# New written orders of all engines in the first five and the last iterations of a two-layer graph-attention kernel

## What is computed

```python
# layer 0
q, k, v = x @ Wq + bq, x @ Wk + bk, x @ Wv + bv
attn = softmax(where(adj == 0, -inf, q k^T / sqrt(32)))
y = (attn v) @ Wo + bo + x
x = layernorm(y) * gamma + beta
# layer 1
nx = layernorm(x) * ln1_g + ln1_b
q, k, v = nx @ wq + bq, nx @ wk + bk, nx @ wv + bv
bias = where(adj > 0, 0.1 * adj * adj, -inf)
attn = softmax(q k^T / sqrt(32) + bias)
x1 = x + (attn v) @ wo + bo
n2 = layernorm(x1) * ln2_g + ln2_b
out = x1 + gelu(n2 @ w1 + b1) @ w2 + b2
```

## Time and profile before

| what | value |
|---|---|
| median of 3 runs | 2076.92 us |
| the profiled execution's own time | 2076.95 us |
| its span, first to last instruction | 2075.2 us |
| TensorE busy | 2028.0 us, 98% |
| VectorE, ScalarE busy | 1655.5 and 1654.2 us, 80% each |
| GpSimd busy | 1005.0 us, 48% |
| mean granted clock of TensorE | 0.99 |
| DMA, mean rate | 35 GB/s |

### The profile page before, as it was taken

One profiled execution on the slowest core, in us unless ns is written; L12 is line 12 of the kernel. 1 busy time (PEld: TensorE's weight loads), 2 busy tenths in 40 slices (PEclk: granted clock), 3 DMA queues, 4 the chain that ended last, 5 costly groups with the idle time before them and its releaser, 6 DMA issues.

```text
span 2075.2 us, 57260 instructions
## 1 busy us (share of the span) xinstructions
PE 2028.0 (98%) x19008; PEld 1782.2 (86%) x19008; DVE 1655.5 (80%) x7107; ACT 1654.2 (80%) x5512; POOL 1005.0 (48%) x780
## 2 busy tenths in 40 slices
...
DMA packets 80830, 73.16 MB, mean 35 GB/s; under 512 B 3024, under 2 KB 72272, under 8 KB 80720
## 3 DMA queue, kind: packets, MB, share of 16 engines
...
q10 hardware_dynamic: 144, 0.01, 0.0%
...
## 4 chain that ended last, share of the span: by engine, by line
PE 96%; DVE 3%; issue 1%; DMA 1%; ACT 0%; SPq 0%; POOL 0%; ACTq 0%; DVEq 0%
PE ps L509 52%; PE ps L519 11%; PE ps L491 11%; PE ps L479 7%; PE ps L502 6%; PE ps L518 5%; PE ps L531 3%; PE ps L521 1%; DVE pm L939 1%; DVE xy L1036 0%; DMA m<-in_adj 0%; DMA xTr<-in_xT 0%; DVE stats L1021 0%; PE ps L463 0%; DVE actl L982 0%
## 5 line engine op out<-in xcount | busy, mean ns | idle before, releaser
L703 ACT ACTIVATE pm<-pm,nmax 128x128 f32<-128x128 f32 x2048 | 793.0, 393 | 97.8 <-DVE nmax L939 97.3
L1180 POOL TENSOR_TENSOR pm<-pm,rinv 128x512 f32<-128x512 f32 x512 | 524.1, 1044 | 715.8 <-DVE rinv L955 715.7
L939 DVE CUSTOM_DVE_ANT_0 pm<-ps,m 128x128 f32<-128x128 f32 x2048 | 452.9, 283 | 21.4 <-PE ps L479 16.0
L703 ACT ACTIVATION_READ_ACCUMULATOR pm<-pm,nmax 128x1 f32 x2048 | 392.7, 192 | 0.0
L519 PE MATMUL ps<-w,hh 128*128 128x512 f32 x1024 | 363.4, 399 | 2.5 <-DVE hl L1043 2.4
L491 PE MATMUL ps<-ident,pm 128*128 128x128 f32 x2048 | 288.9, 277 | 2.7 <-DVE nmax L939 1.9
L491 PEld LDWEIGHTS ps<-ident,pm 128*128 128x128 f32 x2048 | 236.7, 142 | 32.9 <-issue 3.4
L713 ACT ACTIVATE pt<-ps 128x512 f32<-128x512 f32 x256 | 151.2, 591 | 128.4 <-PE ps L491 128.3
L518 PE MATMUL ps<-w,hl 128*128 128x256 f32 x896 | 249.9, 279 | 0.0
L962 DVE COPY pt<-ps 128x512 f32<-128x512 f32 x256 | 169.2, 679 | 66.4 <-PE ps L491 66.2
L519 PEld LDWEIGHTS ps<-w,hh 128*128 128x128 f32 x1024 | 188.0, 188 | 39.1 <-DVE hl L1043 3.1
...
## 6 DMA issues: line engine op xcount, KB each, us to landing
...
```

Source lines behind the costliest of these rows:

```text
L703: last = nc.scalar.activation(pm[:, g, h, :], pm[:, g, h, :], ACT.Exp, bias=nmax[:, g, h:h + 1], scale=-1.0, accum_out=rsum[:, g, h:h + 1])
L939: last = nc.vector.tensor_tensor_reduce(out=pm[:, g, h, :], in0=src[:, at:at + N], in1=m[:, g, :], scale=1.0, scalar=3e38, op0=ALU.add, op ...
L1180: tt(pm[:, g, hs, :], pm[:, g, hs, :], rinv[:, g, hs].rearrange("p (h a) -> p h a", a=1).to_broadcast([P, HC, N]), ALU.mult).then_inc(norm ...
```

## The change

Only orders change. `body(i)`, `JOBS` and every helper stay as they are, as does all of SyncE's program. `head()` and `tail()` of TensorE, ScalarE, VectorE and GpSimd hold the same calls as before in another order, and `HEAD` and `TAIL` follow TensorE's. No instruction is added or removed. The parts of the diff that the prediction speaks of (a deleted and an added run of lines stand apart where lines between them are left out):

```diff
@@ -586,39 +585,39 @@
-                qkv(X, 0, 4); scores(X, 0, 1); flip(X, 0, 0, 0); flip(X, 0, 0, 1); qkv(X, 0, 5); second_products(0)
+                qkv(X, 0, 4); qkv(X, 0, 5); scores(X, 0, 1); flip(X, 0, 0, 0); flip(X, 0, 0, 1); second_products(0)
...
-                qkv(Y, 0, 1); flip(X, 1, 1, 0); qkv(Y, 0, 2); qkv(Y, 0, 3); qkv(Y, 0, 4); scores(Y, 0, 0)
+                flip(X, 1, 1, 0); qkv(Y, 0, 1); qkv(Y, 0, 2); qkv(Y, 0, 3); qkv(Y, 0, 4); scores(Y, 0, 0)
...
-                values(X, 1, 0); values(X, 1, 1); out_proj(X, 1, 0); scores(Y, 0, 1); qkv(X, 2, 0); out_proj(X, 1, 1)
+                values(X, 1, 0); values(X, 1, 1); out_proj(X, 1, 0); scores(Y, 0, 1); out_proj(X, 1, 1); qkv(X, 2, 0)
...
-                flip(Y, 0, 3, 0); flip(Y, 0, 3, 1); values(Y, 0, 0); values(Y, 0, 1); flip_rows("T1", 1, 0)
-                scores(X, 2, 1); flip_rows("T1", 1, 1); flip(X, 2, 0, 0); out_proj(Y, 0, 0); out_proj(Y, 0, 1)
-                flip(X, 2, 0, 1); qkv(Y, 1, 0); qkv(Y, 1, 1); qkv(Y, 1, 2); flip(X, 2, 1, 0); qkv(Y, 1, 3)
+                flip(Y, 0, 3, 0); flip(Y, 0, 3, 1); values(Y, 0, 0); values(Y, 0, 1); scores(X, 2, 1)
+                flip_rows("T1", 1, 0); out_proj(Y, 0, 0); flip(X, 2, 0, 0); flip_rows("T1", 1, 1); flip(X, 2, 0, 1)
+                out_proj(Y, 0, 1); qkv(Y, 1, 0); flip(X, 2, 1, 0); qkv(Y, 1, 1); qkv(Y, 1, 2); qkv(Y, 1, 3)
...
@@ -637,27 +636,27 @@
...
-                mlp_up(29, 3); mlp_up(29, 4); values(X, 31, 0); values(X, 31, 1); mlp_up(29, 5); mlp_up(29, 6)
-                mlp_up(29, 7); out_proj(X, 31, 0); out_proj(X, 31, 1); scores(Y, 30, 1); flip(Y, 30, 0, 0)
-                mlp_down(29, 0); mlp_down(29, 1); flip(Y, 30, 0, 1); flip(Y, 30, 1, 0); mlp_down(29, 2)
...
+                mlp_up(29, 6); out_proj(X, 31, 0); mlp_up(29, 7); scores(Y, 30, 1); out_proj(X, 31, 1)
+                flip(Y, 30, 0, 0); mlp_down(29, 0); mlp_down(29, 1); mlp_down(29, 2); flip(Y, 30, 0, 1)
+                flip(Y, 30, 1, 0); flip(Y, 30, 1, 1); mlp_down(29, 3); flip(Y, 30, 2, 0); flip(Y, 30, 2, 1)
...
@@ -762,36 +761,36 @@
-                x_hi(0, 0); x_hi(0, 1); q_out(X, 0, 0); q_out(X, 0, 1); copy_wo(0); k_out(X, 0, 0); k_out(X, 0, 1)
-                exp(X, 0, 0, 0); exp(X, 0, 0, 1); exp(X, 0, 1, 0); exp(X, 0, 1, 1); copy_pt(X, 0, 0); exp(X, 0, 2, 0)
-                exp(X, 0, 2, 1); exp(X, 0, 3, 0); exp(X, 0, 3, 1); copy_pt(X, 0, 1); copy_pt(X, 0, 2)
-                copy_pt(X, 0, 3); out_hi(X, 0, 0); x_hi(1, 0); x_hi(1, 1); out_hi(X, 0, 1); copy_w2(0); q_out(X, 1, 0)
...
+                x_hi(0, 0); x_hi(0, 1); copy_wo(0); q_out(X, 0, 0); q_out(X, 0, 1); k_out(X, 0, 0); k_out(X, 0, 1)
+                exp(X, 0, 0, 0); exp(X, 0, 0, 1); exp(X, 0, 1, 0); exp(X, 0, 1, 1); copy_pt(X, 0, 0); x_hi(1, 0)
+                exp(X, 0, 2, 0); exp(X, 0, 2, 1); exp(X, 0, 3, 0); exp(X, 0, 3, 1); copy_pt(X, 0, 1); copy_pt(X, 0, 2)
+                x_hi(1, 1); copy_pt(X, 0, 3); out_hi(X, 0, 0); out_hi(X, 0, 1); copy_w2(0); k_out(X, 1, 0)
...
-                out_hi(X, 1, 0); exp(Y, 0, 1, 0); exp(Y, 0, 1, 1); x_hi(2, 1); out_hi(X, 1, 1); exp(Y, 0, 2, 0)
...
+                out_hi(X, 1, 0); x_hi(2, 1); exp(Y, 0, 1, 0); out_hi(X, 1, 1); exp(Y, 0, 1, 1); exp(Y, 0, 2, 0)
...
@@ -1045,63 +1044,64 @@
-                x_lo(0, 0); x_lo(0, 1); split_kv(0, 1); first_rows(0); mask0(0); split_kv(0, 2)
...
-                mask_scores(X, 0, 2, 1); mask_scores(X, 0, 3, 0); split_qkv1(0, 0); recip(X, 0, 2)
-                mask_scores(X, 0, 3, 1); copy_pt(X, 0, 0); v_out(X, 0, 1); recip(X, 0, 3); second_shifts(0)
-                copy_pt(X, 0, 1); copy_pt(X, 0, 2); split_qkv1(0, 1); copy_pt(X, 0, 3); out_lo(X, 0, 0); x_lo(1, 0)
-                x_lo(1, 1); out_lo(X, 0, 1); residual("WO0", 0, 0); mask0(1); residual("WO0", 0, 1); norm_stats(0, 0)
-                norm_rows(0, 0); mask_scores(X, 1, 0, 0); mask_scores(X, 1, 0, 1); mask_scores(X, 1, 1, 0)
-                mask_scores(X, 1, 1, 1); norm_stats(1, 0); v_out(X, 1, 0); v_out(X, 1, 1); recip(X, 1, 0)
-                norm_rows(1, 0); mask_scores(X, 1, 2, 0); lo("T1", 0, 0); lo("T1", 0, 1); recip(X, 1, 1)
-                mask_scores(X, 1, 2, 1); mask_scores(X, 1, 3, 0); copy_pt(X, 1, 0); split_w1(0, 0); recip(X, 1, 2)
-                mask_scores(X, 1, 3, 1); split_w1(0, 1); v_out(Y, 0, 0); mask_scores(Y, 0, 0, 0); recip(X, 1, 3)
-                mask_scores(Y, 0, 0, 1); mask_scores(Y, 0, 1, 0); flipped(X, 1, 1, 1); mask_scores(Y, 0, 1, 1)
-                copy_pt(X, 1, 1); copy_pt(X, 1, 2); copy_pt(X, 1, 3); v_out(Y, 0, 1); out_lo(X, 1, 0); recip(Y, 0, 0)
-                x_lo(2, 0); mask0(2); residual("WO0", 1, 0); recip(Y, 0, 1); x_lo(2, 1); mask_scores(Y, 0, 2, 0)
-                out_lo(X, 1, 1); mask_scores(Y, 0, 2, 1); mask_scores(Y, 0, 3, 0); residual("WO0", 1, 1)
-                recip(Y, 0, 2); norm_stats(0, 1); mask_scores(Y, 0, 3, 1); norm_rows(0, 1); mask_scores(X, 2, 0, 0)
-                mask_scores(X, 2, 0, 1); flipped(Y, 0, 1, 0); mask_scores(X, 2, 1, 0); recip(Y, 0, 3)
-                copy_pt(Y, 0, 0); flipped(Y, 0, 1, 1); mask_scores(X, 2, 1, 1); copy_pt(Y, 0, 1); norm_stats(1, 1)
-                copy_pt(Y, 0, 2); copy_pt(Y, 0, 3); recip(X, 2, 0); norm_rows(1, 1); v_out(X, 2, 0); v_out(X, 2, 1)
...
+                x_lo(0, 0); x_lo(0, 1); first_rows(0); mask0(0); split_kv(0, 1); split_kv(0, 2)
...
+                mask_scores(X, 0, 2, 1); mask_scores(X, 0, 3, 0); mask_scores(X, 0, 3, 1); split_qkv1(0, 0)
+                recip(X, 0, 2); copy_pt(X, 0, 0); v_out(X, 0, 1); second_shifts(0); recip(X, 0, 3); copy_pt(X, 0, 1)
+                copy_pt(X, 0, 2); x_lo(1, 0); copy_pt(X, 0, 3); mask0(1); x_lo(1, 1); out_lo(X, 0, 0); out_lo(X, 0, 1)
+                split_qkv1(0, 1); residual("WO0", 0, 0); residual("WO0", 0, 1); norm_stats(0, 0); norm_rows(0, 0)
+                mask_scores(X, 1, 0, 0); mask_scores(X, 1, 0, 1); mask_scores(X, 1, 1, 0); mask_scores(X, 1, 1, 1)
+                norm_stats(1, 0); v_out(X, 1, 0); v_out(X, 1, 1); norm_rows(1, 0); recip(X, 1, 0)
+                mask_scores(X, 1, 2, 0); recip(X, 1, 1); lo("T1", 0, 0); lo("T1", 0, 1); mask_scores(X, 1, 2, 1)
+                mask_scores(X, 1, 3, 0); split_w1(0, 0); split_w1(0, 1); recip(X, 1, 2); mask_scores(X, 1, 3, 1)
+                copy_pt(X, 1, 0); v_out(Y, 0, 0); mask_scores(Y, 0, 0, 0); recip(X, 1, 3); mask_scores(Y, 0, 0, 1)
+                mask_scores(Y, 0, 1, 0); flipped(X, 1, 1, 1); mask_scores(Y, 0, 1, 1); copy_pt(X, 1, 1)
+                copy_pt(X, 1, 2); copy_pt(X, 1, 3); v_out(Y, 0, 1); out_lo(X, 1, 0); mask0(2); x_lo(2, 0)
+                recip(Y, 0, 0); x_lo(2, 1); residual("WO0", 1, 0); out_lo(X, 1, 1); recip(Y, 0, 1)
+                mask_scores(Y, 0, 2, 0); mask_scores(Y, 0, 2, 1); residual("WO0", 1, 1); norm_stats(0, 1)
+                recip(Y, 0, 2); mask_scores(Y, 0, 3, 0); mask_scores(Y, 0, 3, 1); norm_rows(0, 1); copy_pt(Y, 0, 0)
+                mask_scores(X, 2, 0, 0); mask_scores(X, 2, 0, 1); flipped(Y, 0, 1, 0); mask_scores(X, 2, 1, 0)
+                recip(Y, 0, 3); flipped(Y, 0, 1, 1); mask_scores(X, 2, 1, 1); copy_pt(Y, 0, 1); v_out(X, 2, 0)
+                norm_stats(1, 1); copy_pt(Y, 0, 2); copy_pt(Y, 0, 3); norm_rows(1, 1); v_out(X, 2, 1); recip(X, 2, 0)
+                out_lo(Y, 0, 0); mask_scores(X, 2, 2, 0); lo("T1", 1, 0); out_lo(Y, 0, 1); mask_scores(X, 2, 2, 1)
+                residual("WO1", 0, 0); recip(X, 2, 1); lo("T1", 1, 1); mask_scores(X, 2, 3, 0); residual("WO1", 0, 1)
...
@@ -1124,38 +1124,38 @@
...
-                residual("WO0", 31, 1); norm_stats(0, 31); mask_scores(Y, 30, 2, 0); recip(Y, 30, 1)
-                mask_scores(Y, 30, 2, 1); norm_rows(0, 31); mask_scores(Y, 30, 3, 0); recip(Y, 30, 2)
-                mask_scores(Y, 30, 3, 1); residual_down(29, 0); copy_pt(Y, 30, 0); residual_down(29, 1)
...
+                split_h(29, 5); split_h(29, 6); mask_scores(Y, 30, 2, 0); split_h(29, 7); mask_scores(Y, 30, 2, 1)
+                residual("WO0", 31, 1); recip(Y, 30, 1); norm_stats(0, 31); residual_down(29, 0); recip(Y, 30, 2)
+                norm_rows(0, 31); mask_scores(Y, 30, 3, 0); mask_scores(Y, 30, 3, 1); residual_down(29, 1)
...
+                norm_stats(2, 30); mask1(31); norm_rows(2, 30); mask_scores(Y, 31, 0, 0); mask_scores(Y, 31, 0, 1)
...
@@ -1233,26 +1233,26 @@
...
-                normalise(X, 0, 3, 1); lo_w2(0, 0); root(0, 0); scale_y0(0); shift_y0(0); root(1, 0)
-                normalise(X, 1, 0, 0); normalise(X, 1, 0, 1); add_bo1(0); normalise(X, 1, 1, 0); normalise(X, 1, 1, 1)
...
+                normalise(X, 1, 0, 0); normalise(X, 1, 0, 1); normalise(X, 1, 1, 0); normalise(X, 1, 1, 1)
                 normalise(X, 1, 2, 0); normalise(X, 1, 2, 1); normalise(X, 1, 3, 0); normalise(X, 1, 3, 1); add_bo0(1)
-                normalise(Y, 0, 0, 0); normalise(Y, 0, 0, 1); lo_w2(0, 1); normalise(Y, 0, 1, 0)
...
```

(10 more changed lines are left out.)

316 lines of the change are left out of this document (161 added, 155 removed), and 89 rows, old and new, of tables (HEAD, TAIL).

## The result

The kernel after takes 2063.15 us, the median of 4 runs (2062.86 to 2065.27), against 2077.41 us before (4 runs, 2073.3 to 2078.48). The ratio is 0.9937, with a 95% interval of 0.992 to 0.9954, that is 9.6 to 16.6 us less. The forecast was 2067.1 us, a ratio of 0.9953. The two profiled executions differ by 13.98 us, 2076.95 and 2062.97. The direction was right, and the forecast had about two thirds of the gain.

What follows compares the result with a forecast made beforehand. TensorE was taken to bound the kernel, with no idle time in the loop and gains only in head and tail. The terms summed to 9.8 us less than 2076.95, giving 2067.1 us, range 2061.5 to 2073.

Steps and rivals of the forecast that it cites:

- norm_rows(1, 0), 3.5 us: Head, before flip_rows("T1", 0, 0): rows placed ahead of recip take 1.38 instead of 4.80 us, shrinking the 4.50 us hole by 3.5.
- for the clock: Head, at the norm_rows(1, 0) hole: half-clock time given back, taken as 0.3 us on top of the 3.5.
- x_lo(2, 1), 3.6 us: Head, before qkv(X, 2, 0): the 1.9 us hole goes, and 1.7 us of slow clock behind it.
- norm_rows(1, 1), 1.5 us: Head, before flip_rows("T1", 1, 0): rows placed ahead of recip(X, 2, 0), so the 1.50 us hole goes.
- mask0(3), 1.1 us: Head, before mlp_up(0, 3): moved behind residual("WO0", 2, 0), it no longer waits for its DMA; the 1.08 us hole goes.
- First iteration, 0.5 us: Head, before scores(X, 0, 1): qkv(X, 0, 5) fills the 2.10 us hole; bounds -1.0 and 1.5, 0.5 us taken.
- Tail, 0.6 us: Small holes of 1.8 us go after flip(Y, 30, 0, 1) moves, mostly given back at normalise; 0.6 us taken.
- New waits, -1.3 us: Moved calls may stand behind new waits: 0 to 3 small holes, 0 to 3.2 us, taken as 1.3 us lost.
- the clock comes back too: Rival, chance 0.11: fewer holes also recover a third of 13 us lost to half clock in the head: 2063 us.
- The hold moves: Rival, chance 0.15: lo_w2(0, 0) holds split_qkv1(0, 1), or lo_w2(0, 1) delays root(1, 0); costs 1 to 3 us: 2069.
- Another engine is next in line: Rival, chance 0.16: exponentials, recip and normalise bind behind the holes, half the gain lost in the head: 2072 us.
- slower: Rival, chance 0.04: the loop is entered in another phase and gains a small hole each turn: 2080 us.

Runs made afterwards that it cites:

- hole_filled: Kernel before, all orders kept, with 15 useless TensorE matmuls in the 4.5 us hole before flip_rows("T1", 0, 0): 2073.87 us, ratio 0.999.
- rows10_only: Kernel before with only recip(X, 1, 0) behind norm_rows(1, 0) and add_bo1(0) behind normalise(Y, 0, 0, 0): 2067.86 us, ratio 0.9956.
- rows11_only: Kernel before with only recip(X, 2, 0) moved behind norm_rows(1, 1): 2073.71 us, ratio 0.9992.
- after_again: The kernel after, unchanged, measured again beside few_moves: 2064.82 us, ratio 0.9944 to before.
- three_holds_off: Kernel before, four head calls moved: recip(X, 1, 0) and recip(X, 2, 0) behind their norm_rows, add_bo1(0) later, lo_w2(0, 1) behind shift_y0(0): 2066.12 us.
- tail_only: Kernel before with the new tail of all engines and the old head: 2074.76 us, ratio 0.9995.
- the version with more: Kernel after with both lo_w2 as in hold_moved_on, plus v_out(X, 1, 1) later, q_out(X, 1, 0) and qkv(X, 2, 0) earlier: 2062.42 us.
- xlo_only: Kernel before with only lo_w2(0, 1) moved behind shift_y0(0): 2072.86 us, ratio 0.9984.
- few_moves: Kernel before with the moves of three_holds_off, but add_bo1(0) behind normalise(Y, 0, 1, 1), and mask0(3) behind residual("WO0", 2, 0): 2064.52 us.
- hold_moved_on: Kernel after with lo_w2(0, 0) moved behind shift_y0(0) and lo_w2(0, 1) behind normalise(X, 1, 2, 1): 2064.7 us, ratio 0.994.

## Why the prediction was right, and where it was not

- *norm_rows(1, 0), 3.5 us:* right to 0.1 (the distance from `scores(X, 1, 1)` to `flip_rows("T1", 0, 0)` went from 5.68 to 2.14 us, and 1.0 us of hole was left, as said). The 0.3 us "for the clock" was the mis-sized term: it measured 2.4 us. Shown by hole_filled and rows10_only.
- *x_lo(2, 1), 3.6 us:* right. From `scores(Y, 0, 0)` to `qkv(X, 2, 1)` 19.11 us became 15.62, 3.5 us less, hole and half clock together.
- *norm_rows(1, 1), 1.5 us:* right (1.5 us in rows11_only; 1.2 in the whole change, from `values(Y, 0, 0)` to `qkv(Y, 1, 3)`, between which both orders have the same calls). The half clock at 107 us, ahead of this place, was gone too in the profile of after, for 1.45 us; by after_again this is not the change's doing.
- *mask0(3), 1.1 us:* hole gone, but the term is not the change's alone. In three_holds_off, where `mask0(3)` had not moved, the hole was 0.18 us, and in tail_only, whose head is that of before, 0.33. How long the wait for the load is differs between executions.
- *First iteration, 0.5 us:* nothing. `scores(X, 1, 0)` starts at 51.16 us before and at 51.10 after; from `qkv(X, 0, 4)` to `scores(X, 1, 1)` it is 39.20 us before, 39.16 after and 39.11 in after_again. Of what `qkv(X, 0, 5)` fills, 0.4 us are given back at `k_out(X, 1, 0)`, which now stands ahead of `q_out` (the hole before `scores(X, 1, 0)` grew from 0.87 to 1.25 us, and is 0.87 again in the version with more) and 0.3 at the hold of `split_qkv1(0, 1)`. The rest goes with the clock, which differs between executions: in after_again the head is 0.95 us ahead at `scores(X, 1, 0)`, and has lost it again at `scores(X, 1, 1)`, with a granted clock of 0.58 from 54 to 62 us where before has 0.79.
- *Tail, 0.6 us:* 0.6 on the mean of profiles, and 0.2 in the one profiled execution. It was 1.7 us ahead at `flip(Y, 30, 1, 1)`, and most was given back at `normalise`, as said: the two holes of 0.34 us above end with GpSimd.
- *New waits, -1.3 us:* not in the sum. New holes came, of 0.56 us before `second_products(0)` and 0.41 us before `flip(X, 2, 0, 0)`, but each within a stretch whose other holes shrank by as much.
- *Rivals:* "the clock comes back too" (0.11) is what happened on top of the forecast, and it deserved more: the window of the first 150 us showed 13 us of clock to be had the earlier trace rows, and a window like that of rows 7, laid behind the first hole, would have shown 0.52. The step that was off is "I take 3.5 and 0.3 for the clock". With 2.4 in its place and no new waits the sum is 13.2 us, 2063.8. That this meets 2063.15 so closely is luck in part: the first iteration gave nothing, and the half clock at 107 us and the length of `mask0(3)`'s wait are matters of the execution. "The hold moves" happened and cost 0.3 us, not 1 to 3. "Another engine is next in line" and "slower" did not come: a turn is still 62.40 us.
- *The signs:* `flip_rows("T1", 0, 0)` starts at 61.93 us (62 was said); the three places behind it start 1.7, 3.2 and 2.7 us earlier than said, for the most part by the clock again. No `norm_rows` of the head takes over 1.8 us, and the large holes of the tail are as long as they were.
- *The range:* its ends don't follow from the bounds of the terms. With those that the parts give (0 for `norm_rows(1, 0)`, -1.0 for the first iteration) the low end of the gain is a loss of 0.7 us, not a gain of 3, and the high end is 13.8 us, 2063.2, not 15. The measured gain, 13.98 us in the profiles, is at this upper end; the range of 2061.5 to 2073 held it through the rival at 2063. And of the nine holes that "nearly all end with VectorE" two, of 2.10 and 1.91 us, have no engine to their name in rows 3; for the second the traces show that `x_lo(2, 1)` ended it: in before, three_holds_off, xlo_only and few_moves `qkv(X, 2, 0)` starts 0.1 us after its end.

The rule of the Trainium skill that the prediction weighed (SBUF — State Buffer, section "Who interferes with whom") is borne out here: the SCALAR_TENSOR_TENSOR with two inputs in SBUF was held for 2.0 us, while the four BATCH_NORM_STATS2 of a `norm_stats`, with one input, took 1.40 us beside `lo_w2(0, 1)` and 1.40 us with GpSimd idle. The first two lines are of the kernel after, the last is of hold_moved_on:

```profile
56.37 1.40 DVE L1020 BATCH_NORM_STATS2 stats<-y 128x6 f32<-128x256 f32 x4 [0.35 <-POOL y L1231]
56.29 2.38 POOL L1194 TENSOR_TENSOR w<-pt,w 128x1024 fp32r<-128x1024 f32 x1
...
44.75 1.40 DVE L1020 BATCH_NORM_STATS2 stats<-xy 128x6 f32<-128x256 f32 x4
```

What such a rule can't say is the price, which was 0.3 us at `split_qkv1(0, 1)` and 8 to 9 us at `norm_rows(1, 0)`.
